# Latent attention on one core: both halves of a key tile's weighing directly behind one another

## The reference, cut to what matters

```python
q = (x @ Wq.T).reshape(b, t, N_HEADS, HEAD_DIM).transpose(0, 2, 1, 3)
latent = layernorm(x @ Wdkv.T, ln_g, ln_b)
k = (latent @ Wuk.T)...   # 16 heads of 8
v = (latent @ Wuv.T)...
q, k = apply_rope(q), apply_rope(k)
scores = jnp.einsum('bhqd,bhkd->bhqk', q, k) / np.sqrt(HEAD_DIM)
scores = jnp.where(causal, scores, -jnp.inf)
attn = jax.nn.softmax(scores, axis=-1)
out = jnp.einsum('bhqk,bhkd->bhqd', attn, v)
```

## Time and profile before

| | |
|---|---|
| runs | 1641.85, 1649.71, 1650.86 us |
| span of the profiled execution, first to last instruction | 1651.0 us; no other time of that execution is listed |
| TensorE busy | 1249.1 us (76%) |
| VectorE busy | 1170.6 us (71%) |
| ScalarE busy | 955.1 us (58%) |
| GpSimd busy | 584.3 us (35%) |
| weigh matmuls, L1749 | x4608, 338.3 us busy |
| maxima reductions, L1909 | x1152, 680.9 us busy |
| exponentials, L1850 | x640, 558.5 us busy |

### The profile page before, as it was taken

One profiled execution on the slowest core, in us unless ns is written; L12 is line 12 of the kernel. 1 busy time (PEld: TensorE's weight loads), 2 busy tenths in 40 slices (PEclk: granted clock), 3 DMA queues, 4 the chain that ended last, 5 costly groups with the idle time before them and its releaser, 6 DMA issues. The chain is left out here.

```text
span 1651.0 us, 37456 instructions
## 1 busy us (share of the span) xinstructions
PE 1249.1 (76%) x14319; PEld 665.4 (40%) x14319; DVE 1170.6 (71%) x2634; ACT 955.1 (58%) x1539; POOL 584.3 (35%) x1039
## 2 busy tenths in 40 slices
PE   2755565467767788999999486876878899999948
PEld 2744454366542222223333285653322222233337
DVE  4348698735778989997874354477799999887345
ACT  2225775322345678888888342244556788878822
POOL 2430078245864321221112553285342111111246
PEclk9976665678569999999999786757799999999979
DMA  9252000021000000001010251000000000000023
GB/s 253 78 170 95 1 3 3 25 67 55 1 3 2 1 2 1 1 2 29 2 28 27 59 152 38 2 0 1 1 1 2 2 2 1 2 2 1 2 76 39
DMA packets 56801, 50.80 MB, mean 31 GB/s; under 512 B 7921, under 2 KB 52066, under 8 KB 56178
## 3 DMA queue, kind: packets, MB, share of 16 engines
q1 hardware_dynamic: 48818, 37.77, 8.2%
q0 software_dynamic: 6864, 9.55, 2.3%
q10 hardware_dynamic: 944, 1.10, 0.2%
HBM read 36.16 MB, written 21.35 MB: 35 GB/s over the span
## 5 line engine op out<-in xcount | busy, mean ns | idle before, releaser
L1909 DVE TENSOR_REDUCE arena<-psum 128x1 f32<-128x512 f32 (+4 forms) x1152 | 680.9, 654 | 134.7 <-PE psum L1711 94.3
L1850 ACT ACTIVATE arena<-psum 128x1024 f32<-128x1024 f32 (+3 forms) x640 | 558.5, 900 | 175.6 <-PE psum L1733 167.9
L1749 PE MATMUL psum<-arena 128*9 128x256 f32 (+1 forms) x4608 | 338.3, 375 | 1.0 <-POOL arena L1969 1.0
L1711 PE MATMUL psum<-arena 64*128 64x128 bf16 (+3 forms) x1664 | 223.8, 317 | 91.2 <-DVE arena L1909 80.4
L1733 PE MATMUL psum<-arena 64*128 64x512 bf16 (+3 forms) x1280 | 226.9, 354 | 14.3 <-ACT arena L1850 6.5
L1969 POOL TENSOR_SCALAR_AFFINE_SELECT arena<-arena 128x256 f32<-128x256 f32 x256 | 103.4, 406 | 355.9 <-ACT arena L1850 353.6
L1711 PEld LDWEIGHTS psum<-arena 64*128 64x128 bf16 x1664 | 69.4, 95 | 261.7 <-DVE arena L1909 221.5
L1749 PEld LDWEIGHTS psum<-arena 128*9 128x9 f32 x4608 | 74.5, 89 | 159.7 <-issue 121.3
L1733 PEld LDWEIGHTS psum<-arena 64*128 64x128 bf16 x1280 | 62.9, 94 | 158.1 <-ACT arena L1850 74.6
L1947 POOL CAST arena<-arena 128x16 bf16<-128x16 f32 x64 | 16.3, 254 | 287.3 <-DVE arena L1914 285.3
L698 ACT ACTIVATE small<-psum,YT 128x128 f32<-128x128 f32 x168 | 52.7, 365 | 93.1 <-PE psum L651 93.1
(11 more groups left out here) (368 smaller groups left out, 2074.6 us busy)
## 6 DMA issues: line engine op xcount, KB each, us to landing
regions<-sorted_rows SPq DMA_DIRECT2D x11, 741.8 KB, 14.6
big_w<-in_w SPq DMA_DIRECT2D x2, 2048.0 KB, 20.2
arena<-taps SPq DMA_DIRECT2D x16, 256.0 KB, 3.4
arena<-taps SPq DMA_DIRECT2D x4, 1024.0 KB, 10.6
ACCn<-regions SPq DMA_DIRECT2D x48, 64.5 KB, 1.8
ACCn<-made_rows SPq DMA_DIRECT2D x12, 256.0 KB, 3.7
w<-in_w SPq DMA_DIRECT2D x2, 1024.0 KB
sorted_rows<-arena SPq DMA_DIRECT2D x1, 1483.5 KB, 14.4
```

Of the source, the lines that this page charges most:

```text
L1711: mm = pe.matmul(psum[:, bank_of(("max", (v, m + r))), at:at + w], plain_q[v % 2][rows, a, i * P:(i + 1) * P], keys[rows, 2 * hq + a, key: ...
L1749: mm = pe.matmul(psum[32 * hh:32 * hh + 9, O_BANK, lo:hi], values[:, tile_of(v, j), 4 * hq + hh, :], prob[(t + hh // 2) % N_PROB][:, hh % ...
L1850: act.activation(prob[t % N_PROB][:, :, off:GW], both, ACT.Exp, scale=INV_SQRT_HD).then_inc(a_got, 1)
L1909: dve.tensor_reduce(place, rows, AX.X, ALU.max).then_inc(a_max_got, 1)
```

## The change

Half 1 of a tile's weighing gets the same place as half 0. It used to stand half a step later, except at the last tile of a unit. The sort is stable and keeps the two in this order. Nothing else is changed.

```diff
                 for j in range(TILES_OF[v]):
                     step = 2 * (TILES_TO[v] + j) + (4 if j == 0 else 3)
-                    places += [(half_at[step] + 0.6, "weigh", (v, j, 0))]
-                    places += [(half_at[step + (j < TILES_OF[v] - 1)] + (0.6 if j else 0.3), "weigh", (v, j, 1))]
+                    places += [(half_at[step] + 0.6, "weigh", (v, j, half)) for half in range(2)]
```

## The result

The changed kernel takes 1687.13 us (1683.72 to 1688.99) against 1647.07 us (1641.85 to 1650.86): ratio 1.024, 95% interval [1.020, 1.028]. It is slower by 40 us; the forecast was 1680, slower by 30.

The account below looks back on a forecast made before the run. VectorE's reductions were taken to bound the steady state, at 1.19 us per pair of maxima matmuls against TensorE's 1.09. Two blocks at 13.2 + 2 us give +30 on 1649.7: 1680 us, range 1665 to 1695.

Parts of the forecast that it names:

- VectorE's floor: Steady state: one pair of maxima matmuls (M) to the next takes at least 1.19 us for VectorE; TensorE alone needs 1.09.
- TensorE's saving: At 101 places a block where half weighings become adjacent, TensorE gains 0.12 us plus 0.08 us each.
- The first rival: TensorE is the bound, so 101 adjacent places at 0.20 us save 20 us a block: 1610 us, chance 0.08.
- The sum: Stretches between pairs of maxima, priced at the longer of TensorE's slots and VectorE's floor: +13.2 us a block, ScalarE +2.
- 74 that gain a half: Stretches between pairs of maxima holding one more half weighing: 50 at the floor +16.2 us, 20 TensorE's +8.4, four +1.6.
- 88 that lose their only one: Stretches losing their one half weighing: 32 above the floor fall to it, -6.9 us; 56 at the floor give nothing.
- 44 that hold two both times: Stretches with two half weighings before and after: 0.20 us saved where they become adjacent, -4.6 us together a block.
- ScalarE's term: Where a unit has one maxima pair a tile, two exponentials need 1.84 us: +2 a block, bounds 0 and +10.
- The signs that I named: VectorE's runs split into fours, idle behind maxima up 15 to 20 us; wrong if maxima behind a late pair come under 1.1.
- No new wait, no gain from buffers that come free earlier: Weighing's waits stay on half 0; probability buffers come free half a step earlier, but no exponential waited for them.
- Made up by the next stretch: Rival: with three banks, the next stretch makes up a late pair of maxima; 1645 to 1657 us, chance 0.09.
- Slower still: Rival: adjacent halves starve ScalarE too, +10 us on both blocks and 0.1 per floor stretch; about 1706 us, chance 0.13.

Follow-up runs that it names:

- e1: Kernel before, with VectorE's 512-wide maxima reductions cut to the first 16 keys: 1583.42 us, 0.959 of the kernel before.
- e2: The changed kernel with 512-wide maxima reductions cut to the first 16 keys: 1581.43 us, 0.959 of the kernel before.
- e7: Kernel before, with halves joined in units 0 to 8 only: 1672.78 us, 1.015 of the kernel before.
- e5: Kernel before, with half of ScalarE's full-width exponentials of units 4 to 15 left out: 1640.14 us, 0.997 of the kernel before.
- e6: The changed kernel with half of the full-width exponentials of units 4 to 15 left out: 1663.78 us, 1.013 of the kernel before.
- e3: Kernel before, with joined weighings directly behind a pair of maxima and that stretch's score behind the next pair: 1739.26 us, 1.054 of the kernel before.

## Why the prediction was right

- **VectorE's floor.** The step that carried the forecast: M to M takes 1.17 to 1.19 whatever TensorE does, and a late pair isn't made up. The trace after shows 1.52 and 1.17 in turn. With the floor at 0.66 the stretches that lose their half give back 27 us a block instead of 7 (e1, e2), and the units with many maxima cost 27.1 us of blocks where 26.4 were priced (e7). Right, and shown by experiments.
- **TensorE's saving.** Priced at 0.20 a place: 16 matmuls take 0.98 to 0.99 against two times 0.55. Inside the two blocks TensorE is busy 744.2 us before and 718.1 after, 26 less, where I had named 10 to 30. It is real, and worth nothing where it falls into a wait for VectorE. The first rival (faster, 1610) is refused: the saving that it rested on is there, but even with the floor at 0.66 (e1, e2) joining brings nothing, since 1.52 + 0.66 is 2 x 1.09. What it would bring with no floor at all wasn't run.
- **The sum.** +26.4 priced and +4 for ScalarE; +32.5 measured in the blocks, +30.9 in the spans, +40 in the medians. The classes of stretches have the sizes that I counted, and each came out within 2.4 us of its price:

| stretches of a block | priced | measured, first and second block |
|---|---|---|
| 74 that gain a half | +26.2 | +25.7, +28.4 |
| 88 that lose their only one | -6.9 | -7.4, -7.5 |
| 3 that lose one of several | -1.9 | -1.3, -1.7 |
| 44 that hold two both times | -4.6 | -2.7, -3.0 |
| the others | +0.4 | +2.8, -1.0 |

  The 44 gave 2 us a block less than priced, about what ScalarE's term was put at; with half the exponentials left out (e5, e6) they give 1.4 us a block more in units 10 to 15. The others include units 0 to 3, where the clock moves. I had written that the clock was 0.98 to 1.00 throughout, from windows that begin at 500 us; from 473 to 500 us it is 0.57 before. In the first block after, TensorE's granted clock falls to 0.50 and 0.67, partly or wholly its lower level of 1.2 GHz, from 510 to 530 us (first fence), where it was 1.00 before (second fence):

```profile
500.00:510.00 10.00, 7.19 (x86) 2.31 (x84) 8.92 (x17) 5.48 (x9) 6.80 (x20) 0.99 0.01 2
510.00:520.00 10.00, 8.22 (x64) 3.56 (x64) 6.24 (x12) 3.60 (x5) 2.39 (x7) 0.50 0.00 1
520.00:530.00 10.00, 7.22 (x60) 2.11 (x58) 8.79 (x16) 3.41 (x5) 5.59 (x17) 0.67 0.00 0
```
```profile
510.00:520.00 10.00, 7.00 (x82) 2.48 (x82) 9.51 (x20) 4.20 (x7) 5.17 (x16) 1.00 0.00 0
520.00:530.00 10.00, 8.50 (x113) 3.38 (x111) 8.63 (x17) 6.60 (x11) 4.50 (x12) 1.00 0.01 2
```

  These 20 us lie in units 2 and 3. The stretches of units 0 to 3 that hold as many halves as before grew by 2.1 us there, so the clock explains some 2 of the 4.2 us by which the first block grew more than the 13.2 priced. That is an argument; no run isolated it. I had put nothing on the clock. That the forecast of 1680 missed the median by only 7 us has a share of luck: its base, 1649.7, was above the later median of 1647.1, while the growth of 40 was a third more than the 30 forecast.
- **The signs that I named.** VectorE's runs split into fours, as said. Its idle time behind the maxima between 500 and 900 us went from 44.4 to 49.8 only, not up by 15 to 20; over the whole kernel it went from 94.3 to 111.3. And I had called myself wrong if the M behind a late one came in under 1.1: in each block six do, at 0.88 or 0.89. They are pairs of 256 keys, whose shorter reductions I had priced at a lower floor, so the sign was put too broadly.
- **No new wait, no gain from buffers that come free earlier.** Right: weigh matmuls wait 1.5 us for GpSimd in the whole kernel (1.0 before) and not otherwise, and their weight loads 25.8 us for ScalarE (21.7 before).
- **ScalarE.** Put at +4 in all. e6 leaves the loss standing by 24 to 33 us, so it isn't the cause. By the medians its share could be four times mine; by the stretches of units 10 to 15 it is about 3 us (e5, e6), where I had looked for it. Its waits for scores did grow, by 20 us between 500 and 900 us, but an idle ScalarE that isn't the bound costs nothing.
- **Made up by the next stretch** (no change) is refused by the 23 stretches a block of 1.16 or 1.17 behind a 1.52, and by none of the 26 being shorter. **Slower still** (1706) didn't come; e3 shows that waits for ScalarE cost that much once scores are bunched.

## What to carry to other kernels

Where one in-order engine feeds two others through few buffers, what counts in its order is the work between two hand-overs to the busier consumer, not the sum of its work. Here the consumer had only one pair in reserve, and a burst longer than its period was lost each time, even though it made the feeding engine's own work shorter. To judge such an order, list what stands between hand-overs, take the longer of the producer's slots and the consumer's loop for each, and look for a place in the trace that already has the burst. The same list was used to pick places where bursts are free: it gave 0.5% here, and 1.1% together with the move by 0.4, about 18 of 21 us priced. It held only while the second consumer's events stayed spread.

## What the runs showed that I hadn't expected

With nearly the same priced sum, an order that sets two scores behind one another and the weighing close behind them lost 84 us in the blocks (e3), most of it in waits of 1 to 2 us for ScalarE and GpSimd in the small units. And cutting two thirds of the reductions from 512 to 16 elements only halved VectorE's reduction time, from 680.9 to 306.9 us. The mean of 0.31 us below mixes shapes: the 768 short ones take 98.1 us together, 0.17 each where they took 0.68, and a pair of them 0.26. The other 384, masked or narrower, were not cut and take the remaining two thirds:

```profile
L1911 DVE TENSOR_REDUCE arena<-psum 128x1 f32<-128x16 f32 (+4 forms) x1152 | 306.9, 312 | 413.4 <-PE psum L1711 356.3 <-PE psum L1722 54.0
```
